# A three-stage token mixer on one core: the filter's parameters computed in column groups, and three output banks in the retention stage

## The reference

```python
dt = exp(log_dt); A = -exp(inv_A_real) + 1j * A_imag
dtA = A * dt[:, None]
C = B * C_in * (exp(dtA) - 1.0) / A
K = 2.0 * einsum('chn,hnl->chl', C, exp(dtA[:, :, None] * arange(512))).real
h = K                                            # (16, 192, 512)
# retention, 8 heads, keys 64 wide, values 128 wide, on x = layernorm(h)
q, k = rope(x @ Wq), rope(x @ Wk); v = x @ Wv; g = x @ Wg
scores = einsum('bihd,bjhd->bhij', q * scale, k) * D     # D: causal decay by head
o = einsum('bhij,bjhd->bihd', scores, v)
o = o * rsqrt(mean(o * o) + eps) * g_norm_weight
h = h + (o * silu(g)).reshape(B, T, -1) @ Wo
# top-1 gated shared keys and values, causal softmax attention of 16 heads
h = h + ffn(layernorm(h))
```

## Time and profile before

| what | before |
|---|---|
| median of 3 runs | 1287.13 us |
| the profiled execution's own time | 1287.16 us |
| its span, first to last instruction | 1285.3 us |
| mean granted TensorE clock | 0.989 |
| PE busy | 1190.9 us, 93% |
| DVE busy | 726.2 us, 56% |
| ScalarE busy | 563.3 us, 44% |
| GpSimd busy | 519.6 us, 40% |
| DMA, mean | 120 GB/s |

### The profile page before, as it was taken

How to read it: one execution, slowest core, us unless ns; L and a number is a source line. 1 busy time by engine, 2 the same in 40 slices (tenths; PEclk the granted TensorE clock), 3 DMA queues, 4 the chain that set the end, 5 groups by cost and what they waited for, 6 DMA issues and landing times. The chain is left out here.

```text
span 1285.3 us, 21205 instructions
## 1 busy us (share of the span) xinstructions
PE 1190.9 (93%) x7408; PEld 978.3 (76%) x7408; DVE 726.2 (56%) x1360; ACT 563.3 (44%) x1777; POOL 519.6 (40%) x722
## 2 busy tenths in 40 slices
PE   0389999999999999779999999998999999999997
PEld 0268888888888888668877777787787887878875
DVE  7687656766655742264555555534555656556554
ACT  4444334444334422253333333313555565555656
POOL 2857667667667651142333333302213212232131
PEclk9999999999999999899999999999999999999998
DMA  4132232222222222993676653314606427156061
GB/s 153 56 135 104 91 123 91 107 107 99 107 108 90 107 99 106 300 279 99 213 230 205 197 156 109 90 46 95 132 25 142 104 63 164 50 117 132 12 139 34
DMA packets 63353, 154.68 MB, mean 120 GB/s; under 512 B 9616, under 2 KB 26128, under 8 KB 61712
## 3 DMA queue, kind: packets, MB, share of 16 engines
q1 hardware_dynamic: 63248, 153.33, 40.7%
HBM read 67.19 MB, written 56.62 MB: 96 GB/s over the span
## 5 line engine op out<-in xcount | busy, mean ns | idle before, releaser
L1703 ACT ACTIVATE probs<-psum,row_max 128x128 f32<-128x128 f32 (+1 forms) x384 | 143.2, 389 | 41.1 <-DVE row_max L1872 28.5
L1010 ACT ACTIVATE square_scratch<-psum 128x128 f32<-128x128 f32 x192 | 50.8, 275 | 172.1 <-PE psum L1244 172.1
L2002 POOL TENSOR_TENSOR h_rows<-h_rows,y_normed 128x512 f32<-128x512 f32 x24 | 30.8, 1283 | 203.7 <-DVE y_normed L1888 203.7
L1872 DVE TENSOR_REDUCE row_max<-psum 128x2 f32<-128x384 f32 (+1 forms) x128 | 79.0, 618 | 59.2 <-PE psum L2108 35.7
L1979 POOL TENSOR_TENSOR picked_rows<-picked_rows 128x768 f32<-128x768 f32 (+1 forms) x64 | 61.4, 960 | 98.6 <-DVE picked_rows L1854 94.8
L1184 POOL TENSOR_TENSOR rr<-ss,consts_r 128x3 f32<-128x3 f32 x64 | 13.4, 209 | 197.4 <-ACT square_scratch L1010 192.9
L712 PE MATMUL psum<-m,basis 128*128 128x64 f32 x384 | 48.8, 284 | 43.3 <-POOL basis L664 43.3
L683 POOL TENSOR_TENSOR stage<-stage 128x512 f32<-128x512 f32 x48 | 81.6, 1721 | 14.5 <-DVE stage L565 14.5
L1879 DVE COPY raw_f<-psum 128x512 f32<-128x512 f32 x64 | 44.2, 691 | 70.2 <-PE psum L2121 70.2
L712 PEld LDWEIGHTS psum<-m,basis 128*128 128x128 f32 x384 | 49.7, 203 | 45.0 <-issue 43.3
L570 DVE SCALAR_TENSOR_TENSOR gate_rows<-gate_rows,psum 128x512 f32<-128x512 f32 x48 | 33.0, 688 | 86.3 <-ACT gate_rows L399 86.3
(11 more groups left out here) (279 smaller groups left out, 3535.5 us busy)
## 6 DMA issues: line engine op xcount, KB each, us to landing
qk<-stage SPq DMA_DIRECT2D x24, 512.0 KB, 2.6
v<-stage SPq DMA_DIRECT2D x24, 512.0 KB, 2.6
g<-gate_rows SPq DMA_DIRECT2D x24, 512.0 KB, 2.7
qk_rows<-qk SPq DMA_DIRECT2D x16, 512.0 KB, 7.8
q_stack_even<-q_t_high SPq DMA_DIRECT2D x32, 224.0 KB, 4.8
q_stack_even<-q_t_low SPq DMA_DIRECT2D x32, 224.0 KB, 6.6
q_stack_odd<-q_t_high SPq DMA_DIRECT2D x32, 224.0 KB, 5.5
q_stack_odd<-q_t_low SPq DMA_DIRECT2D x32, 224.0 KB, 6.9
```

Source lines behind the costliest of these rows:

```text
L1010: last = nc.scalar.activation(sqs[:, h % 2, t], psum[:, OB[h % 2], t * RV:(t + 1) * RV], ACT.Square, accum_out=ss[:, h % 2, t:t + 1])
L1703: last = nc.scalar.activation(pr[:, g % 2, c], psum[:, SB[g % 3], c], ACT.Exp, bias=mx[:, g % 3, x:x + 1], accum_out=dsum[:, t, h:h + 1])
L1872: V.reduce_max(mx[:, g % 3, 0:nh], psum[:, SB[g % 3], 0:nh * w].rearrange("p (h n) -> p h n", h=nh), AX, negate=True).then_inc(s_max.sem, 1)
L2002: G.tensor_tensor(h, h, yn[:, (NT * i + t) % 2].rearrange("p h f -> p (h f)"), ALU.add).then_inc(added.sem, 1)
```

## The change

In stage P: the parameters are computed in groups of 32 channels (`GC`), six in all, each of 24 steps on tiles of 128x32 or 128x64 in buffers of their own. Group 0 comes first, group 1 in the slot of unit 1, groups 2 to 5 in the slots of units 3, 7, 11 and 15, in front of the ropes. The slots of units -4 to 0 are replaced by an opening written out for each engine (`first`), in which DVE also makes the first corners and two of the basis sums. Each weight has a raw buffer of its own, so that all six loads are issued in the beginning; the memory is that of its low part. `spectrum` of unit 1 stands behind unit 0's Q projection, that of unit 2 behind unit 1's.

In stage Q: output banks 4, 5 and 6 in turn, `scores(i, m + 1)` directly behind `values(i, 2 * m)`, the masks on DVE one step ahead of the gates, and the loads of gates for pair 0 behind those of q and k for pair 1.

```diff
+GC = 2 * HCH
-LEAD = 4
-    w_pairs = [(sb(n + "_high", [P, KC, D], F32R), sb(n + "_low", [P, KC, D], F32R)) for n in names]
+    for n in names:
+        w_hi.append(sb(n + "_high", [P, KC, D], F32R))
+        with ExitStack() as under:
+            w_raw.append(under.enter_context(nc.sbuf_tensor(n + "_raw", [P, KC, D], F32)))
+        w_lo.append(sb(n + "_low", [P, KC, D], F32R))
...
-    g4 = sb("g4", [P, 4, T])
+    g4 = sb("g4", [P, 2, 4, GC])
...
         def load_w(n):
-            if n >= 2:
-
-                sp.wait_ge(w_high, n - 1)
-                sp.wait_ge(w_low, n - 1)
-            sp.dma_start(raw[:, n % 2], d["w_r"][n]).then_inc(w_in[n % 2], 16)
+            sp.dma_start(w_raw[n][:, :, :], d["w_r"][n]).then_inc(w_in[n], 16)
...
         load_w(0)
+        load_c((0, 0))
         load_w(1)
-        load_c((0, 0))
+        sp.dma_start(ident[:, :], d["ident"]).then_inc(const_in, 16)
         load_c((0, 1))
-        sp.dma_start(ident[:, :], d["ident"]).then_inc(const_in, 16)
+        load_w(2)
+        load_w(3)
         sp.dma_start(rope_t[:, :, :].rearrange("p u f -> p (u f)"), d["rope"]).then_inc(const_in, 16)
-        for n in range(2, NP):
-            load_w(n)
+        load_w(4)
+        load_w(5)
```

ScalarE's opening:

```diff
+        def first():
+            trigonometry((0, 0))
+            w_copy(0)
+            digits((0, 0))
+            for n in range(1, NP):
+                w_copy(n)
+            k_evac((0, 0))
+            angle_size((0, 1))
+            h_evac((0, 0))
+            sines((0, 1))
+            norm((0, 0))
+            x_split((0, 0))
+            decay_exp((0, 1))
+            k_evac((0, 1))
+            digits((0, 1))
+            h_evac((0, 1))
+            norm((0, 1))
+            v_evac((0, 0), 0)
+            v_evac((0, 0), 1)
+            x_split((0, 1))
+            g_tanh((0, 0), 0)
```

DVE's group, cut (13 of the 24 steps are left out), its place, and its opening:

```diff
+        def group(k):
+            cols = slice(k * GC, (k + 1) * GC)
...
+            if k >= 2:
+                dve.wait_ge(xy_ready.sem, chunk_at(xy_ready, (0, 2 * k - 3), 1))
+            step(V.tensor_tensor(x(0), ar, ar, ALU.mult))
+            step(V.tensor_tensor(y(0), ai, ai, ALU.mult))
+            step(V.tensor_tensor(x(1), x(0), y(0), ALU.add))
+            step(V.reciprocal(y(1), x(1)))
+            step(V.tensor_scalar(x(0), y(1), 2.0, None, ALU.mult))
...
+            step(V.tensor_tensor(both(5), both(4), bcast(b0, 1, 2), ALU.mult))
+            step(V.tensor_tensor(both(6), both(4), bcast(b1, 1, 2), ALU.mult))
+            step(V.tensor_tensor(x(7), x(5), y(6), ALU.subtract))
+            step(V.tensor_tensor(y(7), y(5), x(6), ALU.add))
...
+            step(V.tensor_scalar(out[:, 0], out[:, 2], sign, -1.0, ALU.mult, ALU.mult))
+            step(V.tensor_scalar(out[:, 1], out[:, 3], sign, None, ALU.mult))
...
+            if u[1] % 4 == 3 and valid(step_of(u, 5)):
+                group((u[1] + 5) // 4)
             if valid(u):
                 rope(u, 0)
                 rope(u, 1)
...
+            if u == (0, 1):
+                scale((0, 2))
+                group(1)
+                x_split((0, 2))
...
+        def first():
+            group(0)
+            scale((0, 0))
+            corners(dve, V, (0, 0))
+            build((0, 0))
+            basis_add(dve, V, (0, 0))
+            reduce((0, 1))
+            row_stats((0, 0))
+            dve.wait_ge(rstd.sem, rstd.of((0, 0), 1))
+            split_weights(0)
+            x_split((0, 0))
+            build((0, 1))
+            basis_add(dve, V, (0, 1))
+            split_weights(1)
+            scale((0, 1))
+            split_weights(2)
+            split_weights(3)
+            dve.wait_ge(const_in, 32)
+            row_stats((0, 1))
+            rope((0, 0), 0)
+            build((0, 2))
+            split_weights(4)
+            rope((0, 0), 1)
+            split_weights(5)
+            x_split((0, 1))
+            build((0, 3))
+            gates((0, 0), 0)
+            reduce((0, 2))
```

GpSimd's and PE's openings:

```diff
+        def first():
+            decay((0, 0))
+            moving((0, 0))
+            decay((0, 1))
+            moving((0, 1))
+            scales((0, 0))
+            moving((0, 2))
+            basis_add(pool, G, (0, 2))
+            rope_add((0, 0), 0)
+            rope_add((0, 0), 1)
+            moving((0, 3))
+            basis_add(pool, G, (0, 3))
+            decay((0, 2))
...
+        def first():
+            u, nxt = (0, 0), (0, 1)
+            spectrum(u)
+            row_transposes(u)
+            x_transposes(u)
+            pe.wait_ge(x_low.sem, x_low.of(u, 1))
+            project(u, WQ, 0).then_inc(qk_sum.sem, 1)
+            spectrum(nxt)
+            project(u, WK, 1).then_inc(qk_sum.sem, 1)
+            row_transposes(nxt)
+            project(u, WV, 2).then_inc(v_sum.sem, 1)
+            project(u, WV + 1, 3).then_inc(v_sum.sem, 1)
+            x_transposes(nxt)
+            pe.wait_ge(roped.sem, roped.of(u, 1))
+            project(u, WG, 4).then_inc(g_sum.sem, 1)
+            pe.wait_ge(roped.sem, roped.of(u, 2))
+            project(u, WG + 1, 5).then_inc(g_sum.sem, 1)
```

Stage Q:

```diff
-    OB = [5, 6]
+    OB = [4, 5, 6]
...
         load_v(sp, 0, 2)
-        for t in range(2):
-            load_g(sp, 0, t)
...
         units["g_stored"](sp)
-        load_g(sp, 0, 2)
+        for t in range(NT):
+            load_g(sp, 0, t)
...
             masked(i, 1)
             if back:
                 y_split(i - 1, 0, 1)
+            masked(i, 2)
             gate_o(i, 0)
...
             for m in range(1, HG):
-                masked(i, 2 * m)
+                masked(i, 2 * m + 1)
                 gate_o(i, 2 * m - 1)
-                masked(i, 2 * m + 1)
+                if m < HG - 1:
+                    masked(i, 2 * m + 2)
                 gate_o(i, 2 * m)
...
-            pe.wait_ge(y_ready.sem, y_ready.at(i, h - 1))
+            pe.wait_ge(y_ready.sem, y_ready.at(i, h - 2 if h >= 2 else h - 1))
...
             values(i, 0)
+            scores(i, 1)
...
             for m in range(1, 3):
-                scores(i, m)
                 if back:
                     wo(i - 1, m - 1, 0)
                 values(i, 2 * m)
+                scores(i, m + 1)
...
-            scores(i, 3)
             if back:
                 wo(i - 1, 2, 0)
...
             i = PAIRS - 1
+            pe.wait_ge(y_ready.sem, y_ready.at(i, RH - 1))
             f["x_transposes"](0, 0)
```

230 lines of the change are left out of this document (114 added, 116 removed).

## The result

| | before | after |
|---|---|---|
| median | 1287.08 us (4 runs, 1285.77 to 1287.61) | 1272.92 us (4 runs, 1271.96 to 1274.81) |
| ratio | | 0.9893, 95% interval 0.9876 to 0.9910 |
| profiled execution, span | 1287.16, 1285.3 us | 1273.32, 1271.5 us |

The kernel is 1.1% faster. The forecast, 1260.6 us, is 12.3 us too low, and the time lies outside the range of 1252 to 1269.

The account below looks back on a forecast made before the run. TensorE, busy 1190.9 of 1285.3 us, was taken as the bound, so only its standing or low-clock time could be won. 1287.16 - 17 (opening) - 9.5 (second stage's first slot) + 0 (other slots) = 1260.6 us; range 1252 to 1269.

Parts of the forecast that it names:

- The walk to unit 0: First-stage opening: smaller parameter groups and earlier weight loads start unit 0's Q at 40.5 us, 22.7 us earlier.
- What unit 0 then waits for: First stage: weight splits on DVE, 5 us in series with GpSimd, make unit 0 take 32 us; unit 2 starts at 93.3.
- Term 1: First-stage opening: unit 2 starts at about 93.3 instead of 110.50, -17 us (bounds -23 to -12).
- The later groups: First stage: groups 2 to 5 put 6.1 us of DVE work before the ropes in four units; cost 0, at most 4 us.
- Term 2: First slot of the second stage: earlier rows and masks save 9.5 us (bounds -4 to -12).
- the walk itself: First slot of the second stage, step by step: its end, slot 1's scores, comes at 557 instead of 566.97.
- Term 3: The seven other slots of the second stage: no change, 0 (bounds -2 to +3 us).
- `gate_o` waits for them 1 us: First slot of the second stage: `gate_o` could start at 540 but waits 1 us for gates landing at about 541.
- the 28 us: Second stage: sign of being wrong if slot 1's scores come later than this after slot 0's (34.5 before, 24.6 forecast).
- R1: Opening: the lock makes DVE and GpSimd one engine, saving only 12 to 13 us there, total 1265; chance 0.13.
- R2: Transition to the second stage is bound by its loads, first slot saves only 4 us, total 1266; chance 0.13.
- R4: Second stage: scores ahead stall at 24 masks, slower; at 2 us each 48 us, total 1309; chance 0.03.

Follow-up runs that it names:

- no_later: The changed kernel without parameter groups 2 to 5 (columns 64 to 191 use the second group's parameters): 1267.23 us, 0.9850 of the kernel before.
- group_first: The changed kernel with each later parameter group ahead of `row_stats` in its slot instead of behind it: 1266.60 us, 0.9846 of the kernel before.
- q_only: The kernel before with only the second stage changed, the opening as it was: 1278.52 us, 0.9937 of the kernel before.
- p_only: The kernel before with only the first stage changed, the second stage as it was: 1279.97 us, 0.9948 of the kernel before.
- gf_mask: group_first with the mask of head 3 made ahead of the gating of head 0 in the second stage's first slot: 1269.10 us, 0.9857 of the kernel before.
- gf_adds: group_first with `basis_add` of units 2 and 3 on VectorE instead of GpSimd: 1266.57 us, 0.9846 of the kernel before.
- gc_adds: group_first with three parameter groups of 64 columns and `basis_add` of units 2 and 3 on VectorE: 1264.48 us, 0.9835 of the kernel before.
- gf_no_splits: group_first with the splits of weights 3 to 5 done on one column in 512, leaving out their low parts: 1264.06 us, 0.9829 of the kernel before.

## Why the prediction was wrong, step by step

- **The walk to unit 0** was right: first matmul at 27.70 (forecast 27), the group done at 18.92 (18.7), the five weight copies at 30.98 (31.0), unit 0 at 41.52 (40.5).
- **What unit 0 then waits for.** The sum was near, its parts were not. Forecast: unit 0 takes 32 us, unit 1 20.9, unit 2 starts at 93.3. Measured: 24.9, 28.5, 94.94. I put 5 us of waiting between VectorE and GpSimd, and 1.5 us for the rows of unit 1, in front of the last weight split, and had it done at 70. It was done at 63.45: VectorE's steps there took 0.7 us more than alone, and it was GpSimd that was slowed (a corner product of 0.30 us took 2.35 beside a split). The series came behind it, in unit 1: there half a `build`, `reduce` and GpSimd's rope sums, `moving` and `basis_add` stood in each other's way, TensorE stood 4.16 us for `basis_add` and then ran at the lower clock for 6.8. That the two errors nearly cancel in the start of unit 2 is luck. Off by 1.6 us.
- **The sum stopped one unit early.** "Unit 2 starts at about 93.3 where it was 110.50" became Term 1 as if unit 2 itself cost what it did. It takes 24.18 instead of 19.14: 1.54 us of waiting for `basis_add` on GpSimd, 3.4 us of low clock. Off by 5.0 us, and in no bound. In the eight other kernels with this opening unit 2 took 21.4 to 23.3 us, so of the 5.0 us 2.3 to 4.2 came in those executions, and the rest belongs to this one.
- **"The later groups ... I take 0; if that cover is gone ... 4 us" is the step that failed most**: 6.2 us (shown by `no_later` and undone by `group_first`). I looked only at the first reader, the G projection, which indeed doesn't wait; and the bound of 4 us was too narrow as well. The late work came out again behind the last of the chain, through GpSimd's operations and the series with `reduce`, in front of the next-but-one unit.
- Together: Term 1 was -17 and is -4.3, and 1.6 + 5.0 + 6.2 = 12.8 us is the whole error: 1260.6 + 12.8 = 1273.4, where the profiled execution took 1273.32. It comes out so only because the errors of the other terms cancel.
- **Terms 2 and 3** were right in sum by luck. Forecast -9.5 and 0; slot 0 gave 5.2, the later slots 3.1 and the third stage, which I held to be untouched, 1.2, together 9.5. Term 2 was 4.3 us too large (the walk itself, 557 for 566.97, gives 10.0 and not 9.5), and Term 3 lies outside its own bounds of -2 to +3. The wait for rows fell as forecast (under 1 us). "`gate_o` waits for them 1 us" was 3.88 us, the waits of TensorE for masks came to 7.3 us where I had about 3, and slot 0 took 29.3 and not 24.6, past the 28 us that I had named as a sign of being wrong. Slot 1 gave 1.3 us and the later ones 0.4 to 0.5 each from slot 3 on, where I had put nothing. `q_only` has the slots of 36.8 us too and `p_only` doesn't, so the edits of the second stage did that; which of them, no run shows.
- **The range** had no room for this: its upper end of 1269 stands for R1 and R2 with the clock, and has nothing for a unit behind unit 2 or for the later groups. The worst bounds of the three terms (-12, -4 and +3) add up to 1274, so the range was narrower than my own bounds allow.
- **Rivals.** R1 named the right mechanism: the two engines work in series where they meet. But its 1265 stopped at unit 2 as well. R2, that the transition is bound by its loads, fits the first slot, where new orders of the loads moved the waits and not their sum; no run proves it. R4's stalls in all slots didn't come (0.26 us a slot). The rule of the Trainium skill (SBUF — State Buffer, "Who interferes with whom"), by which two such operations exclude each other for the whole instruction, agrees with the trace here: 2.65 us against 0.63 alone, and the splits of 4 elements, which end with the GpSimd operation beside them. But the page has it for VectorE operations with two inputs in SBUF (and some others), so it doesn't put all work of the two engines in series, as the prediction took it: VectorE's gating step at 68.94, which reads PSUM, kept its 0.68 us beside a rope sum.

Open: why `gf_mask` varies so; what `p_only` does in its faster executions; and how much of slot 0 would go if fewer bytes had to come between 517 and 530 us, since no run changed that amount.

## What to carry to other kernels

Work put in front of a chain can cost at the end of the chain, not at its first reader: follow the displaced work through every engine to the point where it meets the next unit's work, and place it where its engine idles (here 2.47 us ahead of `row_stats`; that alone was worth 6 us). When a start is moved forward, carry the sum on until the units are undisturbed again, since here the units behind the earlier start were the longer ones (28.5 and 24.2 us instead of 19.2). Where two engines work in series, moving work from one to the other may only change which wait is seen: `gf_adds` alone brought nothing here. It brought 5.0 us at the start of unit 3 once other work had left the same stretch (`gc_adds`). And count what an edit really leaves out: a short operation that waits for the other engine costs as much as a long one.

## What the runs showed of the hardware

A wait of TensorE may or may not be followed by the lower clock, and its length doesn't tell. All kernels here with the opening of the changed kernel wait in unit 2. In the changed kernel 1.54 us of waiting were followed by 6.8 us at 0.50 (unit 2: 24.18 us), first windows. In `gf_mask` and `group_first` 1.53 and 1.84 us were followed by none (22.0 and 22.3), and in five others 1.90 to 2.28 us by 3.4 us at 0.50 (22.9 to 23.3). The window of `group_first` comes second. In the kernel before, waits of 4.64 us at 51.58 and of 4.18 at 63.21 were followed by none, third, where the 4.16 us in unit 1 of the changed kernel were by 6.8:

```profile
103.40:106.80 3.40, 3.40 (x15) 3.11 (x15) 3.26 (x7) 0.00 (x0) 0.81 (x3) 0.50 0.00 0
106.80:110.20 3.40, 3.40 (x10) 2.63 (x9) 3.40 (x8) 2.48 (x3) 3.24 (x5) 0.50 0.01 2
110.20:113.00 2.80, 2.80 (x14) 2.27 (x13) 2.02 (x1) 2.77 (x5) 2.80 (x2) 1.00 0.37 151
```

```profile
102.30:116.80 14.50, 13.51 (x69) 11.15 (x69) 13.21 (x18) 8.65 (x14) 11.68 (x12) 1.00 0.18 73
```

```profile
51.60:63.20 11.60, 5.52 (x24) 4.93 (x24) 4.54 (x7) 7.63 (x10) 7.08 (x13) 1.00 0.05 6
63.20:80.00 16.80, 16.14 (x68) 13.04 (x68) 16.59 (x13) 4.32 (x3) 6.72 (x3) 1.00 0.49 169
```

So traces of the same opening differ by up to 2.7 us in one unit, as much as several of the edits here were to bring. And an operation of one engine can be long only because it waits for the other: a split of 4 elements took 1.02 and 1.21 us beside GpSimd operations that ended with it, and 0.27 elsewhere (`gf_no_splits`).
